# MLP to experts: row turning, early loads and the second slot's gate splits moved

## The reference, cut to what matters

```python
# inside the Mamba block, at its end (h is the normalised x)
mlp = silu(h @ w1.T) * (h @ w3.T) @ w2.T          # D_FF = 2048
x = x + (x1 + mlp)                                # the outer and the inner residual
# mixture of experts
h = layernorm(x)                                  # over the 512 columns
logits = h @ router_w.T                           # 16 experts
top_vals, top_idx = top_k(logits, 2); gates = sigmoid(top_vals)
gate, up = split(h @ gate_up_w[e]); out_e = (silu(gate) * up) @ down_w[e]
moe = sum of gates * out_e over a token's two experts
shared = (silu(h @ sg.T) * (h @ su.T)) @ sd.T     # hidden width 1024
x = x + moe + shared
```

## Time and profile before

| | |
|---|---|
| median of 3 runs | 2533.22 us (2531.15 to 2533.98) |
| the profiled execution's own time | 2530.96 us |
| its span, first to last instruction | 2529.1 us |
| TensorE busy | 2395.7 us (95%) |
| DVE busy | 1978.0 us (78%) |
| ACT busy | 1604.4 us (63%) |
| POOL busy | 679.5 us (27%) |
| mean granted TensorE clock | 0.980 |

### The profile page before, as it was taken

One profiled execution on the slowest core, in us unless ns is written; L12 is line 12 of the kernel. 1 busy time (PEld: TensorE's weight loads), 2 busy tenths in 40 slices (PEclk: granted clock), 3 DMA queues, 4 the chain that ended last, 5 costly groups with the idle time before them and its releaser, 6 DMA issues. The chain is left out here.

```text
span 2529.1 us, 39410 instructions
## 1 busy us (share of the span) xinstructions
PE 2395.7 (95%) x14143; PEld 1014.8 (40%) x14143; DVE 1978.0 (78%) x1982; ACT 1604.4 (63%) x1973; POOL 679.5 (27%) x468
## 2 busy tenths in 40 slices
PE   7999999999999799999999999999887778998999
PEld 3333333333333244444444444444332223444554
DVE  5777777777777788888888888888679993267996
ACT  5555555565555477887888787887384441237994
POOL 1455555565555400000000000000029990010001
PEclk9999999999999899999999999999889988999999
DMA  6245644554445593433333342432340005148994
GB/s 249 87 149 169 203 158 149 167 171 160 149 148 151 141 260 84 116 98 102 92 105 95 99 105 80 120 94 85 114 167 1 0 5 195 51 161 329 405 405 172
DMA packets 178205, 366.02 MB, mean 145 GB/s; under 512 B 19545, under 2 KB 90329, under 8 KB 174425
## 3 DMA queue, kind: packets, MB, share of 16 engines
q1 hardware_dynamic: 176610, 360.81, 44.9%
q0 software_dynamic: 1280, 4.20, 0.5%
q10 hardware_dynamic: 248, 0.15, 0.0%
HBM read 254.24 MB, written 106.68 MB: 143 GB/s over the span
## 5 line engine op out<-in xcount | busy, mean ns | idle before, releaser
L466 DVE TENSOR_REDUCE kv_mx<-kv_s 128x1024 f32 (+1 forms) x512 | 595.4, 1218 | 222.7 <-PE kv_s L502 222.7
L818 DVE TENSOR_TENSOR at_pl<-at_pf,at_ph 128x1024 f16<-128x1024 f32 x512 | 613.1, 1223 | 113.7 <-ACT at_ph L765 104.8
L771 ACT ACTIVATE at_pf<-at_st 128x1024 f32<-128x1024 f32 x512 | 497.4, 1026 | 187.0 <-PE at_st L939 176.4
L938 PE MATMUL at_st<-keep_big,at_k_cur 128*128 (+1 forms) x1024 | 390.5, 381 | 10.1 <-DMA keep_big<-q_dram 7.1
L939 PE MATMUL at_st<-keep_big,at_k_one 128*128 (+1 forms) x1024 | 389.0, 380 | 0.0
L765 ACT ACTIVATE at_ph<-at_pf 128x1024 f16<-128x1024 f32 x256 | 273.2, 1067 | 0.0
L1135 POOL MEMSET mamba_zero<- 128x2 f32 x1 | 0.1, 100 | 939.7 <-POOLq L60 939.7
L900 PE MATMUL at_acc<-at_ph,at_vs 128*128 128x512 f16 x1024 | 242.4, 379 | 2.7 <-DVE at_pl L818 2.6
L382 POOL TENSOR_TENSOR kv_ksl<-kv_kf,kv_ksh 128x512 f16<-128x512 f32 x128 | 148.0, 1156 | 246.4 <-ACT kv_ksh L410 246.4
L1049 PE MATMUL kv_kp<-first_ch,first_wkh 128*128 128x512 f16 x512 | 195.2, 381 | 4.5 <-DVEq L448 4.5
L407 ACT ACTIVATE kv_kf<-kv_kp,first_bks 128x512 f32<-128x512 f32 x128 | 87.4, 683 | 170.0 <-PE kv_kp L1049 170.0
(11 more groups left out here) (357 smaller groups left out, 3884.8 us busy)
## 6 DMA issues: line engine op xcount, KB each, us to landing
keep_big<-gate_up SPq DMA_DIRECT2D x17, 2048.0 KB, 12.1
at_vs<-vd SPq DMA_DIRECT2D x64, 512.0 KB, 3.9
at_k_cur<-kd SPq DMA_DIRECT2D x126, 256.0 KB, 3.9
vd<-kv_vs SPq DMA_DIRECT2D x15, 2048.0 KB
kv_tf<-wpack SPq DMA_DIRECT2D x21, 1024.0 KB, 9.4
keep_big<-down SPq DMA_DIRECT2D x17, 1024.0 KB
first_cf<-ctxT SPq DMA_DIRECT2D x16, 1024.0 KB, 12.3
ex_yg<-gate_up SPq DMA_DIRECT2D x8, 2048.0 KB, 13.1
```

The source lines that it names most:

```text
L466: nc.vector.reduce_max(mx[:, bass.ds(g * (NH * TT) + 2 * (m - TT), 2)], s1[:, m % 3, :, :], AX.X).then_inc(s1_max, 1)
L771: nc.scalar.activation(pf[:, s % FULL, :, :], st[:, s % HP % NST, :, :], ACT.Exp, scale=SCORE).then_inc(pf_ready, 1)
L818: nc.vector.tensor_tensor(pl[:, s % RING, :, :], pf[:, s % FULL, :, :], ph[:, s % RING, :, :], ALU.subtract).then_inc(pl_ready, 1)
L938: nc.tensor.matmul(st[:, w % NST, e, :], k_cur[:, tile], qh[:, q], start=True, stop=False)
```

## The change

In `gated_mlp`, SP also loads set 1 (the first expert) and the router's halves (now keep.router) behind the shared set. TensorE turns keep_a in the MLP's block: tiles 0 to 2 in the last token tile's W2 products, ahead of step j = 10, tile 3 at the end; the turned rows go to gp and up. ACT and DVE make hh and hl there, two chunks at a time. In `experts` the transposes, hh, hl, the router's loads and the loads of set 1 are gone. The gates of set 2 are split at the end of shared(0), beside the down products, rather than in slot 0. ACT waits for smf_ready before a slot's Silu.

```diff
         next_in, next_h, next_l = m.sem("next_in"), m.sem("next_h"), m.sem("next_l")
+        expert_in, a_ready = m.sem("expert_in"), m.sem("a_ready")
+        hT_ready, hh_ready, hl_ready = m.sem("hT_ready"), m.sem("hh_ready"), m.sem("hl_ready")
+        hT = (gp, up)
         g_ready, u_ready, sg_ready, mf_ready, mh_ready, ml_ready = (
...
+            sp.dma_start(ex.gf[1], gate_up[0:D, :].rearrange("(c p) n -> p c n", p=P)).then_inc(expert_in, 16)
+            sp.dma_start(ex.df[1], down[0:EH, :].rearrange("(c p) n -> p c n", p=P)).then_inc(expert_in, 16)
+            at = DIC * 64
+            for s, r in enumerate(keep.router):
+                sp.dma_start(r.rearrange("p c n -> p (c n)"),
+                             wsplit[s][:, W.SMALL[0], at:at + DC * NE]).then_inc(expert_in, 16)
             sp.wait_ge(next_in, 32)
+            sp.wait_ge(expert_in, 64)
...
                 nc.scalar.activation(rows.sd[:, ts], rows.var[:, ts], ACT.Sqrt).then_inc(sd_ready, 1)
+                tok = slice(ts.start * P, ts.stop * P)
+                for k in range(2):
+                    act.wait_ge(hT_ready, 2 * n + k + 1)
+                    nc.scalar.activation(keep.hh[:, 2 * k:2 * k + 2, tok], hT[k][:, :, tok], ACT.Copy,
+                                         scale=SA).then_inc(hh_ready, 1)
...
+            def halves(n, ts):
+                tok = slice(ts.start * P, ts.stop * P)
+                for k in range(2):
+                    dve.wait_ge(hh_ready, 2 * n + k + 1)
+                    nc.vector.scalar_tensor_tensor(keep.hl[:, 2 * k:2 * k + 2, tok], hT[k][:, :, tok], SA,
+                                                   keep.hh[:, 2 * k:2 * k + 2, tok], ALU.mult,
+                                                   ALU.subtract).then_inc(hl_ready, 1)
...
                 for t in range(ts.start, ts.stop):
-                    own.inc(nc.vector.tensor_scalar(keep.a[:, t, :], keep.x1[:, t, :], rows.mv[:, t, 0:1],
-                                                    rows.rs[:, t:t + 1], ALU.subtract, ALU.mult))
+                    nc.vector.tensor_scalar(keep.a[:, t, :], keep.x1[:, t, :], rows.mv[:, t, 0:1],
+                                            rows.rs[:, t:t + 1], ALU.subtract, ALU.mult).then_inc(a_ready, 1)
+                halves(n, ts)
...
                         ).then_inc(u_ready, 1)
+            def turn(ts):
+                pe.wait_ge(a_ready, ts.stop)
+                for k in range(2):
+                    for c in range(2):
+                        for t in range(ts.start, ts.stop):
+                            last = nc.tensor.transpose(hT[k][:, c, t * P:(t + 1) * P],
+                                                       keep.a[:, t, (2 * k + c) * P:(2 * k + c + 1) * P],
+                                                       keep.ident[:, :])
+                    last.then_inc(hT_ready, 1)
...
                         pe.wait_ge(ml_ready, j + 1)
+                    if t == TT - 1 and j == 10:
+                        turn(parts[0])
                     last = product(nc, op[:, t, :], three(mh[:, j, tok], ml[:, j, tok], w2h[:, j, :], w2l[:, j, :]),
                 last.then_inc(o_ready, 1)
+            turn(parts[1])
...
         mh, ml = (m.sb(n, [P, EHC, T], F16) for n in ("mh", "ml"))
-        rh, rl = (m.sb(n, [P, DC, NE], F16) for n in ("rh", "rl"))
+        rh, rl = keep.router
         ident = keep.ident
...
         x_in = [m.sem(f"x_in{i}") for i in range(RX)]
-        w_in, made, consts = m.sem("w_in"), m.sem("made"), m.sem("consts")
-        hT_ready, hh_ready, hl_ready, l_ready = (m.sem(n) for n in ("hT_ready", "hh_ready", "hl_ready", "l_ready"))
+        made, consts = m.sem("made"), m.sem("consts")
+        l_ready = m.sem("l_ready")
         lg_ready, sig_ready, ah_ready, al_ready = (m.sem(n) for n in ("lg_ready", "sig_ready", "ah_ready", "al_ready"))
...
-            return w // 3 + (w % 3 > 0)
+            return w // 3 + (w % 3 > 1)
...
         def _(sp):
-            at = DIC * 64
-            for s, r in enumerate((rh, rl)):
-                sp.dma_start(r.rearrange("p c n -> p (c n)"), wsplit[s][:, W.SMALL[0], at:at + DC * NE]).then_inc(w_in, 16)
             gates_of = gate_up.rearrange("(e c p) n -> p e c n", p=P, c=DC)
...
-            load_gates_up(1)
-            load_down(1)
             load_gates_up(2)
...
                 par = w % 2
-                if cs[0] == 0:
+                if cs[0] == 0 and arrivals(w):
                     act.wait_ge(g_in[w % 3], 16 * arrivals(w))
...
             def down_in(w):
-                act.wait_ge(d_in[w % 3], 16 * arrivals(w))
+                if arrivals(w):
+                    act.wait_ge(d_in[w % 3], 16 * arrivals(w))
...
                 act.wait_ge(sg_done, s + 1)
+                if s:
+                    act.wait_ge(smf_ready, s)
                 nc.scalar.activation(ssg[:, :], sgp, ACT.Silu, scale=UNSCALE).then_inc(ssg_ready, 1)
...
                     act.wait_ge(su_ready, s)
-                split_gates(w + 1, (0, 1, 2, 3))
+                if s:
+                    split_gates(w + 1, (0, 1, 2, 3))
                 if s + 1 < SLOTS:
...
-            for c in range(DC):
-                act.wait_ge(hT_ready, c + 1)
-                nc.scalar.activation(keep.hh[:, c, :], op[:, c, :], ACT.Copy, scale=SA).then_inc(hh_ready, 1)
             nc.scalar.activation(ah[:, :, 0, :], keep.a[:, :, :], ACT.Copy, scale=SA).then_inc(ah_ready, 1)
...
+            act.wait_ge(u_ready, EHC)
+            split_gates(2, (0, 1, 2, 3))
             rows(0)
...
                     low_slot(s - 1)
-                split_gates(w + 1, (0, 1))
+                    split_gates(w + 1, (0, 1))
                 dve.wait_ge(su_ready, s + 1)
...
                     add(0)
-                split_gates(w + 1, (2, 3))
+                else:
+                    split_gates(w + 1, (2, 3))
                 split_down(w + 1, 0)
...
-            for c in range(DC):
-                dve.wait_ge(hh_ready, c + 1)
-                nc.vector.scalar_tensor_tensor(keep.hl[:, c, :], op[:, c, :], SA, keep.hh[:, c, :],
-                                               ALU.mult, ALU.subtract).then_inc(hl_ready, 1)
             choose()
...
             shared(0)
+            split_gates(2, (0, 1, 2, 3))
             for s in range(SLOTS):
...
-            transpose_rows(nc, keep.a, op, ident, hT_ready)
-            pe.wait_ge(w_in, 32)
-            pe.wait_ge(hl_ready, DC)
             for t in range(TT):
...
         keep.ident = m.sb("ident", [P, P])
+        keep.router = [m.sb(f"router{i}", [P, DC, NE], F16) for i in range(2)]
         attention(nc, keep, x, q_dram, m_dram, mrow, m_out, kd, vd, sums, r_dram, bv, bo, n1w, wsplit, xs_dram)
             m = Space(nc, inner, "mamba")
```

## The result

Over 11 executions each on one chip, the changed kernel took 2526.69 us (median; 2524.60 to 2528.73), the kernel before 2533.02 (2530.85 to 2536.26): 6.3 us less, a ratio of 0.9979 with a 95% interval of 0.9971 to 0.9987. A second comparison on another chip (last experiment) gave 2528.38 against 2532.51, ratio 0.9985 (0.9976 to 0.9994). The profiled execution took 2526.69 with a span of 2524.6; before it was 2530.96 and 2529.1.

What follows compares the result with a forecast made beforehand. TensorE, always busy in the experts' steady part, was taken as the bound, so gains lie before it. Slot 0's -0.65 and the second slot's -3.79 gave -4.44: 2528.8 us from median 2533.22, range 2527 to 2531 (all cases 2526 to 2532.4).

Steps and rivals of the forecast that it cites:

- Twelve transposes, 1.32: MLP's last token block: twelve transposes moved among the W2 products add 1.32 us to TensorE; the halves after them stay hidden.
- The router's start: Boundary between MLP and experts: the router's products start near 2248.5 against 2250.26, TensorE 1.76 us earlier.
- DVE's choice: Opening of the experts' block: DVE's choice of experts, waiting for POOL's constants, starts at 2250.56 against 2251.99, 1.43 us earlier.
- The clock's return: After the boundary: TensorE's clock falls again; its return may cost 1.5 us, but no difference was taken.
- The loads, "nothing alone": Router weights and first expert's matrices loaded in the MLP: nothing at the boundary waited for them, so worth nothing alone.
- The scatter, 0.8: Before slot 0: DVE's moved splits slow POOL's last two scatter issues, 2.4 to 4.0 us together; price 0 to 1.6, taken 0.8.
- Rival A: Before slot 0: the scatter is not held up, gain 5.2 us, 2528.0; chance 0.25.
- The second slot, 3.79: First expert slots: with splits done beside the down products, slot 2 follows at 2303.05 against 2306.84, 3.79 us earlier.
- B: Before slot 0: POOL issues its last scatter only after DVE's splits, -0.7 in all, 2532.5; B and C together 0.15.
- C: Steady expert slots: saturated DMA loads give the time back, 0.1 beyond the slack loses 1.8 (2530.6); B and C together 0.15.
- D: Shared gate and up products: the clock stays at 1.2 GHz, 15 us slower, 2548; with other slower cases 0.06.
- E: Beside the shared down products: ACT and DVE are too busy to split there; chance 0.02.

Runs made afterwards that it cites:

- last experiment: The changed kernel unchanged, run again beside the kernel before on one chip: 2528.38 against 2532.51 us, ratio interval 0.9976 to 0.9994.
- splits alone: Kernel before, with only the second slot's gates split beside the shared down products: 2528.49 against 2531.49 us (0.9979 to 0.9997).
- the turn alone: Changed kernel, but set 1 loaded and set 2's gates split where they were before: 2533.04 against 2531.49 us (0.9996 to 1.0014).

## Why the prediction was right, point by point

- **Twelve transposes, 1.32.** The last tile's sum comes 11.60 after the mark against 10.29: 1.31. The halves were hidden, with 1.88 of idle left on DVE; their 256-column operations took 0.38 and 0.42, as taken.
- **The router's start.** Expected 1.76 sooner, it was 2.1: the clock fell only behind the last four transposes, not ahead of them, and they ran at full speed (0.44 for two with the filling).
- **DVE's choice.** Expected 1.43, was 1.66 sooner, for the same reason; the wait for POOL's constants was there (0.48).
- **The clock's return.** This is a term that was mis-sized: I took no difference, the first product lost 0.94 more than before (4.85 against the 3.91 of the earlier trace rows in the chain of waits), inside the bound of 1.5. The return hardly moved with the router's start (23.7 after the mark, 23.9 before). The prediction had DVE as the last at the end of the shared products, 1.43 sooner. It was TensorE, as before: DVE's wait for its last up product was 0.33 and is 0.83, and that wait ends 1.16 sooner.
- **The loads, "nothing alone".** Right alone and wrong in company. I had looked for who waits for these loads and not for what they stand ahead of in the DMA queues, and I had the block's later opening in the sum without asking what it does to the loads behind it. In the sum no term changed by it, since the change moves them.
- **The scatter, 0.8.** The tie of the earlier trace rows was real and the hold-up too, but this term was mis-sized: the last two issues took 3.11 together (2.55 without the splits), not up to 4.0, and where a hold-up of 1.0 was measured (splits alone) its effect on the landing was 0.1 to 0.3. Slot 0 came 1.22 sooner, not 0.65. The two errors, clock (1.16 where 1.43 was taken) and scatter (next to nothing where 0.8 was), partly cancel there, which is luck; both chains end within 0.2 of each other. Rival A's outcome (5.2) was nearer than my forecast (4.4), but not for its reason: the issues were held up. The Trainium skill, page "SBUF — State Buffer", section "Who interferes with whom", has the contention of two-input vector instructions with a GpSimd instruction that reads SBUF; the runs agree for the splits (1.43 to 1.97 beside them, 0.97 with DVE idle, and again 0.97 where only DVE's wait was added). Not every such instruction costs an issue time: in the changed kernel an issue of 0.97 (2273.85) ran beside the low half ex_ml (0.68, two SBUF inputs). Its inference that making descriptors is spared did not save these indirect issues; whether their descriptors or their reading of the places waited, no run here shows.
- **The second slot, 3.79.** 3.79 in every trace with the splits moved. The near-tie at the last split (0.3) that I had feared cost nothing.
- **Rivals B to E.** B is refuted by the issues' 1.44 and 1.97. C: in the steady part DMA is as full as before, 404 GB/s; the load that takes 12.0 in the earlier trace rows takes 11.9. Slack stays, since loads are issued by events of their slots. D: the clock was back within the first product each time at this place; its danger was real at another, the first slots (3.5 us in the turn alone). E is excluded by DVE's splits at 2276.47. The Trainium skill, page "TensorE: Matmul & The Clock Gate", section "HAM oscillation — how this bites in real kernels", puts the fall down to waits for data that are long enough; here the longest hole ahead of the first fall was 1.12 us, and holes of 2.35 in the kernel before brought none, so one hole's length doesn't decide in these traces.
- **The number.** The forecast was 2528.8 with 2527 to 2531 for itself and 2526 to 2532.4 for all of its cases; the median of 2526.69 lies in the second range and just under the first, and that of the repeat, 2528.38, in both. The gain was forecast as 4.4, is 5.0 in the traces and 6.3 and 4.1 in the medians. 2526.5 for the profiled execution and 2526.69 measured agree by luck: the span ahead of the mark was 0.57 longer, and the gain behind it 0.6 larger. From the median of before, 2533, the traces' 5.0 give 2528.0; measured 2526.69 and, beside 2532.51, 2528.38.

## What to carry to other kernels

Look for operations that sit in an engine's list ahead of what another engine waits for, and move them to where that engine is idle: for the second slot this could be worked out to a hundredth. Where a tie stands in the trace, price what comes second, since two near-ties (clock and scatter here) leave only the smaller gain. An edit that is worth nothing alone can be what lets another one count: here the earlier loads keep the DMA engines free for the scatter, and with the moved splits the clock fell in the slots in none of eight traces. When work moves across a block boundary, ask also what the later opening does to the loads issued behind it.

## What the runs showed of the hardware that I had not expected

- The clock fell in the midst of products, after two holes of 1.01 or 1.08 and 1.12 us, in both executions of the same kernel, while longer holes (2.35, 1.89) in the kernel before left it at 2.4 GHz in two executions. One such fall cost 1.5 us, two 3.5.
- The first 2230 us varied by 7 us over 14 profiled executions (granted clock 0.98 over that stretch in each), while distances behind the mark came again within 0.11 in the changed kernel and 0.15 in the turn alone; in the kernel before, M1 differed by 0.41 (SP's row load by 0.14).
- A POOL issue that DVE's splits made 1.0 longer delayed the load behind it by 0.1 to 0.3 only.
